# The query-key-value projection of each node tile done in slots inside the pooling stage of a two-layer graph network

## The reference

```python
h = jnp.maximum(_layernorm(x, axis=-1), 0.0)
x = x + _L0_gnn_ref(h, W1, w2, src, dst)     # pooling: a softmax per dst of tanh(h @ W1.T) @ w2 at src, weights for h[src]
h = jnp.maximum(_layernorm(x, axis=-1), 0.0)
x = x + _L1_gnn_ref(h, edge_index, edge_attr_16, ...)
# _L1: two TransformerConv layers (8 heads of 16, then 1 head of 128)
q, k, v = x @ Wq + bq, x @ Wk + bk, x @ Wv + bv
alpha = sum(q[dst] * (k[src] + e)) / sqrt(C)     # e = edge_attr @ We
out = segment_sum((v[src] + e) * softmax_per_dst(alpha)) + x @ Ws + bs
```

## Time and profile before

| what | us |
|---|---|
| median of 3 timed runs (10591.73 to 10635.79) | 10591.98 |
| span of the profiled execution | 7414.1 |
| time of the runs that lies outside such a span | 3177.9 |
| GpSimd busy in the span | 4576.5 |
| VectorE busy in the span | 4663.7 |
| TensorE busy in the span | 5718.3 |

### The profile page before, as it was taken

One profiled execution on the slowest core, in us unless ns is written; L12 is line 12 of the kernel. 1 busy time (PEld: TensorE's weight loads), 2 busy tenths in 40 slices (PEclk: granted clock), 3 DMA queues, 4 the chain that ended last, 5 costly groups with the idle time before them and its releaser, 6 DMA issues. The chain is left out here.

```text
span 7414.1 us, 172328 instructions
## 1 busy us (share of the span) xinstructions
PE 5718.3 (77%) x38285; PEld 4085.0 (55%) x38285; DVE 4663.7 (63%) x12926; ACT 3438.6 (46%) x8180; POOL 4576.5 (62%) x4707
## 2 busy tenths in 40 slices
PE   4555566666665688888888888856889999999998
PEld 3455555555542466666666666633555556666666
DVE  4444555555665788999999999933444555555542
ACT  3233333333443466666666666612444444444441
POOL 0777777777750477777666665502777777777630
PEclk7777878888986799999999999977999999999995
DMA  2334444444434666666655555534445555555532
GB/s 81 85 82 83 85 85 87 88 89 89 92 90 140 161 155 157 159 158 153 151 144 145 142 140 137 130 103 119 108 110 112 117 116 119 123 122 123 119 88 60
DMA packets 1267854, 861.45 MB, mean 116 GB/s; under 512 B 637234, under 2 KB 1158320, under 8 KB 1266840
## 3 DMA queue, kind: packets, MB, share of 16 engines
q1 hardware_dynamic: 1091672, 438.53, 25.3%
q0 software_dynamic: 175168, 411.90, 23.7%
HBM read 780.46 MB, written 69.42 MB: 115 GB/s over the span
## 5 line engine op out<-in xcount | busy, mean ns | idle before, releaser
L757 POOL DMA_INDIRECT ring_multi<-kv_rows,src_cols x1564 | 1609.3, 1029 | 1029.7 <-issue 440.4
L1155 POOL DMA_INDIRECT ring_single<-h_rows,src_cols x1564 | 1482.6, 948 | 857.2 <-issue 480.3
L1155 POOL DMA_INDIRECT ring_pool<-pool_rows,src_cols x1564 | 1482.0, 948 | 678.6 <-issue 451.5
L1258 PE MATMUL ps_s_pool<-ident,row_pool 128*128 128x128 f32 x1952 | 365.1, 319 | 718.0 <-ACT row_pool L1300 716.8
L1300 ACT ACTIVATE row_pool<-ring_pool 128x520 f32 x488 | 309.1, 633 | 1162.1 <-POOLq L1146 1162.1
L958 PE MATMUL ps_e_multi<-w_edge,attrT 64*128 64x512 f32 x976 | 544.5, 638 | 331.4 <-DVE kv L847 310.9
L1222 DVE CUSTOM_DVE_ANT_0 masked_pool<-mask_pool,ps_s_pool,start_pool 128x512 f32<-128x512 bf16 x488 | 364.8, 748 | 633.4 <-PE ps_s_pool L1258 552.3
L1271 PE MATMUL ps_p_pool<-row_pool,probT_pool 128*128 128x129 f32 x3904 | 667.1, 325 | 55.2 <-DVE probT_pool L1235 54.2
L847 DVE TENSOR_TENSOR kv<-ring_multi,ps_e_multi 128x1024 f32<-128x1024 f32 x488 | 596.1, 1222 | 161.6 <-issue 124.0
L1258 PEld LDWEIGHTS ps_s_pool<-ident,row_pool 128*128 128x128 f32 x1952 | 254.1, 160 | 801.5 <-issue 764.9
L1305 ACT ACTIVATE rowT<-ps_r 128x512 f32<-128x512 f32 x488 | 291.7, 598 | 816.4 <-PE ps_r L1265 816.4
(11 more groups left out here) (218 smaller groups left out, 12218.1 us busy)
## 6 DMA issues: line engine op xcount, KB each, us to landing
dst_pool<-in_dst_rows SPq DMA_DIRECT2D x488, 128.0 KB
dst_multi<-in_dst_rows SPq DMA_DIRECT2D x488, 128.0 KB
dst_single<-in_dst_rows SPq DMA_DIRECT2D x488, 128.0 KB
query_multi<-query_parts SPq DMA_DIRECT2D x488, 96.0 KB
cols<-query_cols SPq DMA_DIRECT2D x488, 64.0 KB
ring_pool<-pool_rows,src_cols POOLq DMA_INDIRECT x1564
ring_multi<-kv_rows,src_cols POOLq DMA_INDIRECT x1564
ring_single<-h_rows,src_cols POOLq DMA_INDIRECT x1564
```

What stands on the lines that cost most here:

```text
L757: pool.indirect_dma_start(out=ring[:, u, j, :], out_offset=None, in_=rows, in_offset=bass.IndirectOffsetOnAxis(ap=g.src_cols[:, c:c + 1], ...
L1155: pool.indirect_dma_start(out=ring[:, u, j, :], out_offset=None, in_=rows, in_offset=bass.IndirectOffsetOnAxis(ap=g.src_cols[:, c:c + 1], ...
L1258: i = T_.transpose(ps_s[p1][:, j * P:(j + 1) * P], row[:, u1, j, D + 1:D + 2].to_broadcast([P, P]), g.ident[:])
```

## The change

The projection no longer has a stage. `pool_stage` replaces `dense_stage("pool")`: the same items, with *slots* between them. A slot does one whole tile. There is a slot after every fourth item up to item 387 (97 slots), and one after every item from 390 to 487 (98 slots). Which tile a slot takes is worked out in `prepare`: the next one, if it is finished by then, else the last one again, or the unused 99th tile while none is finished; a slot does its full work in every case. The slot's work is spread over later steps: sums, statistics and `x` at two steps behind the slot's item, normalization at 5, turning at 7 and 9, product at 10, evacuation at 11, the query's parts at 11 and 14, the three stores at 23. The bias is added by a second product of 3 bfloat16 rows. The reciprocal root is an exponential of a logarithm. `skip` and `x1` are stored side by side, and the fold stage loads them with one DMA.

The diff, cut to its core (the removed `project_stage` stands above in full):

```diff
+SLOT_ITEMS = [*range(3, BLOCKS - 1, 4), *range(BLOCKS - 1, ITEMS)]
+TILE_SLOTS = len(SLOT_ITEMS)
+EARLY_SLOTS = len(range(3, BLOCKS - 1, 4))
+SLOT_XB = 4
+SLOT_OB = 16
@@ build
-        dense_stage(g, "pool", g.pool_rows, D + 2, 8)
-        project_stage(g)
+        slot_signals(g)
+        pool_stage(g)
@@ buffers
-    g.kv_rows = scratch("kv_rows", [NODES, 2 * D])
+    g.kv_rows = scratch("kv_rows", [SLOTS * P, 2 * D])
+    g.skip_x_rows = scratch("skip_x_rows", [SLOTS * P, 2 * D])
-    g.x1_rows = scratch("x1_rows", [NODES, D])
-    g.skip1_rows = scratch("skip1_rows", [NODES, D])
@@ prepare, vector: the tile of each slot
+            v.tensor_copy(tiles_done[0:1, 0:EARLY_SLOTS],
+                          item_t[0:1, 4:4 + 4 * EARLY_SLOTS].rearrange("a (s k) -> a s k", k=4)[:, :, 0])
+            v.tensor_copy(tiles_done[0:1, EARLY_SLOTS:TILE_SLOTS - 1], item_t[0:1, BLOCKS:ITEMS])
...
+            v.tensor_tensor_scan(turn[:], ones_slot[:], tiles_done[:], 0.0, ALU.add, ALU.min).then_inc(s_dve, 1)
...
+            v.tensor_copy(g.slot_tiles[:], turn[:]).then_inc(s_dve, 1)
@@ pool_stage: the items as in dense_stage, fully unrolled, with the parts below
+    LAST = ITEMS + 24
...
+        @block.sync
...
+                if has(n, ITEMS):
+                    E["mask"].wait(sp, n - U)
+                    sp.dma_start(dst[:, u], t["dst_rows"][ds(items.block(u), 1), :].to_broadcast([P, EDGES_B]))\
...
+                s = slot_at(n - 8)
+                if s is not None:
+                    tiles[s] = slot_tile(sp, s)
+                    F["x_sum"].wait(sp, s - SLOT_XB)
+                    sp.dma_start(xb[:, s % SLOT_XB], ...
+                s = slot_at(n - 23)
+                if s is not None:
+                    at = ds(tiles.pop(s), 1)
+                    rows_stored(sp, s - 1)
+                    F["x_sum"].wait(sp, s)
+                    F["kvs"].wait(sp, s)
+                    sp.dma_start(g.kv_rows..., out[:, s % SLOT_OB, D:3 * D]).then_inc(stored[s % 2], 16)
+                    sp.dma_start(g.skip_x_rows..., out[:, s % SLOT_OB, 3 * D:5 * D]).then_inc(stored[s % 2], 16)
+                    F["part2"].wait(sp, s)
+                    sp.dma_start(g.parts[D]..., parts[:, s % SLOT_OB]...).then_inc(stored[s % 2], 16)
...
+            def statistics(s):
...
+                tile = ds(slot_tile(dve, s), 1)
+                E["summed"].wait(dve, SLOT_ITEMS[s])
...
+                V.tensor_scalar(den[:, k], weight, 1e-30, None, ALU.max).then_inc(F["weight"].sem, 1)
+                F["weight"].wait(dve, s)
+                V.reciprocal(den[:, k], den[:, k]).then_inc(F["den"].sem, 1)
+                x_landed(dve, s)
+                rows_stored(dve, s - SLOT_OB)
+                F["den"].wait(dve, s)
+                V.scalar_tensor_tensor(out=x1, in0=sums, scalar=den[:, k], in1=x, op0=ALU.mult, op1=ALU.add)\
+                 .then_inc(F["x_sum"].sem, 1)
+                F["x_sum"].wait(dve, s)
+                V.bn_stats(stat[:, k], x1).then_inc(F["stats"].sem, 1)
+                F["stats"].wait(dve, s)
+                V.bn_aggr(agg[:, s % 8], stat[:, k]).then_inc(F["var"].sem, 1)
+
+            for n in range(LAST):
...
+                step(n, n % U)
+                s = slot_at(n - 2)
+                if s is not None:
+                    statistics(s)
+                s = slot_at(n - 5)
+                if s is not None:
+                    F["rstd"].wait(dve, s)
...
+                    V.tensor_scalar(normal[:, s % 2], out[:, s % SLOT_OB, 4 * D:5 * D], agg[:, s % 8, 0:1],
+                                    rstd[:, s % 4], ALU.subtract, ALU.mult).then_inc(F["normal"].sem, 1)
+                s = slot_at(n - 11)
...
+                    V.tensor_tensor(out=rest[:, s % 4], in0=out[:, s % SLOT_OB, 0:D], in1=parts[:, s % SLOT_OB, 0],
+                                    op=ALU.subtract).then_inc(F["rest"].sem, 1)
+                s = slot_at(n - 14)
...
+                    V.tensor_tensor(out=parts[:, s % SLOT_OB, 2], in0=rest[:, s % 4], in1=parts[:, s % SLOT_OB, 1],
+                                    op=ALU.subtract).then_inc(F["part2"].sem, 1)
@@ tensor, between the items' parts
+                s = slot_at(n - 7)
...
+                    T_.transpose(ps_h[:, 0:P], normal[:, s % 2], g.ident[:]).then_inc(F["turned"].sem, 1)
...
+                s = slot_at(n - 10)
...
+                    F["turned_sb"].wait(pe, s)
+                    F["kvs"].wait(pe, s - 1)
+                    T_.matmul(ps_z[:], hT[:, s % 4], w[:].rearrange("p a n -> p (a n)"), start=True, stop=False)
+                    T_.matmul(ps_z[:], ones3[:], bias_rows[:], start=False, stop=True).then_inc(F["product"].sem, 1)
@@ scalar, between the items' two exponentials and the copy of the gathered rows
+            act.preload_act_table_set("natural_log_exp_and_others")
...
+                s = slot_at(n - 9)
...
+                    S_.activation(hT[:, s % 4], ps_h[:, 0:P], ACT.Relu).then_inc(F["turned_sb"].sem, 1)
+                s = slot_at(n - 5)
...
+                    S_.activation(log[:, s % 4], agg[:, s % 8, 1:2], ACT.Ln, bias=g.ln_eps[:]).then_inc(F["log"].sem, 1)
+                    F["log"].wait(act, s)
...
+                    S_.activation(rstd[:, s % 4], log[:, s % 4], ACT.Exp, scale=-0.5).then_inc(F["rstd"].sem, 1)
+                s = slot_at(n - 11)
...
+                    F["product"].wait(act, s)
+                    rows_stored(act, s - SLOT_OB)
+                    S_.activation(out[:, s % SLOT_OB, 0:4 * D], ps_z[:], ACT.Copy).then_inc(F["kvs"].sem, 1)
+                    F["kvs"].wait(act, s)
+                    S_.activation(parts[:, s % SLOT_OB, 0], out[:, s % SLOT_OB, 0:D], ACT.Copy)\
+                     .then_inc(F["part0"].sem, 1)
+                s = slot_at(n - 14)
...
+                    S_.activation(parts[:, s % SLOT_OB, 1], rest[:, s % 4], ACT.Copy).then_inc(F["part1"].sem, 1)
@@ fold_stage, sync
-                    sp.dma_start(skip[:, u], rows_of(g.skip1_rows, n)).then_inc(loaded[u], 16)
-                    sp.dma_start(x1[:, u], rows_of(g.x1_rows, n)).then_inc(loaded[u], 16)
+                    sp.dma_start(skip_x[:, u], rows_of(g.skip_x_rows[0:NODES], n)).then_inc(loaded[u], 16)
```

More of the change, by code:

```diff
@@ L60 @@
 DEN_EPS = 1e-16
+SLOT_ITEMS = [*range(3, BLOCKS - 1, 4), *range(BLOCKS - 1, ITEMS)]
+TILE_SLOTS = len(SLOT_ITEMS)
+EARLY_SLOTS = len(range(3, BLOCKS - 1, 4))
+SLOT_OF = {item: s for s, item in enumerate(SLOT_ITEMS)}
+SLOT_XB = 4
+SLOT_OB = 16
+assert SLOT_ITEMS[EARLY_SLOTS:] == list(range(ITEMS - NODE_TILES, ITEMS))
 assert ITEMS % U == 0 and NODE_TILES % ROWS_B == 0 and BATCHES % 2 == 0
@@ L175, in buffers @@
     g.block_ends = sb(g, ctx, "block_ends", [1, 392], I32)
+    g.slot_tiles = sb(g, ctx, "slot_tiles", [1, TILE_SLOTS], I32)
     g.ident_b = sb(g, ctx, "ident_b", [P, P], BF16)
@@ L222, in prepare @@
         word = sb(g, ph, "word", [1, GROUPS])
+        tiles_done = sb(g, ph, "tiles_done", [1, TILE_SLOTS])
+        ones_slot = sb(g, ph, "ones_slot", [1, TILE_SLOTS])
+        turn = sb(g, ph, "turn", [1, TILE_SLOTS])
+        idle = sb(g, ph, "idle", [1, TILE_SLOTS])
         iota_ni = sb(g, ph, "iota_ni", [P, P], I32)
@@ L364, in _ @@
             v.tensor_scalar(g.fresh_tile[:], ps_b[:, 0:ITEMS], FAR, None, ALU.mult).then_inc(s_dve, 1)
+            v.tensor_copy(tiles_done[0:1, 0:EARLY_SLOTS],
+                          item_t[0:1, 4:4 + 4 * EARLY_SLOTS].rearrange("a (s k) -> a s k", k=4)[:, :, 0])
+            v.tensor_copy(tiles_done[0:1, EARLY_SLOTS:TILE_SLOTS - 1], item_t[0:1, BLOCKS:ITEMS])
+            v.memset(ones_slot[:], 1.0)
+            v.memset(tiles_done[0:1, TILE_SLOTS - 1:TILE_SLOTS], float(NODE_TILES)).then_inc(s_dve, 1)
+            dve.wait_ge(s_dve, done + 16)
+            v.tensor_tensor_scan(turn[:], ones_slot[:], tiles_done[:], 0.0, ALU.add, ALU.min).then_inc(s_dve, 1)
+            dve.wait_ge(s_dve, done + 17)
+            v.tensor_scalar(idle[:], turn[:], 0.0, float(NODE_TILES + 1), ALU.is_equal, ALU.mult).then_inc(s_dve, 1)
+            dve.wait_ge(s_dve, done + 18)
+            v.scalar_tensor_tensor(out=turn[:], in0=turn[:], scalar=-1.0, in1=idle[:], op0=ALU.add, op1=ALU.add)\
+             .then_inc(s_dve, 1)
+            dve.wait_ge(s_dve, done + 19)
+            v.tensor_copy(g.slot_tiles[:], turn[:]).then_inc(s_dve, 1)
         @block.tensor
@@ L442, in _ @@
                 D_["stats"].wait(sp, n - LOADS)
-                sp.dma_start(acc[:, n * ROWS_B:(n + 1) * ROWS_B, 0:D], rows_of(t["x"], n))\
+                sp.dma_start(acc[:, n * ROWS_B:(n + 1) * ROWS_B, 0:D], rows_of(t["x"][0:NODES], n))\
                   .then_inc(loaded[n % LOADS], 16)
@@ L1087, in dense_signals, with slot_signals @@
     g.flat = {k: Signal(sem(g, "flat_" + k)) for k in DENSE_SIGNALS}
+SLOT_SIGNALS = ("weight", "den", "x_sum", "stats", "var", "log", "rstd", "normal", "turned", "turned_sb", "product", "kvs", "part0",
+                "rest", "part1", "part2")
+def slot_signals(g):
```

(15 more changed lines are left out.)

404 lines of the change are left out of this document (245 added, 159 removed).

## The result

| | before | after |
|---|---|---|
| median of the timed runs, us | 10591.85 (4 runs) | 10905.15 (4 runs) |
| span of the profiled execution, us | 7414.1; in e1 10518.7 | 10887.8 |

The ratio is 1.031 (95% interval 1.026 to 1.036). The prediction was 10423.

The account below looks back on a forecast made before the run. The prediction took GpSimd's gathers to set the pooling stage's length, with VectorE narrowest in late items. Its terms, -297 + 78 + 49 + 8 - 10 + 3, summed to -169 us: 10423 us, range 10350 to 10560.

Parts of the forecast that it names:

- rival 5: Whole program: time outside the span grows with some 16,000 more instructions at 18 ns each, +290, 10713 us; chance 3%.
- (a): Removed projection stage: the time between its ends is saved, -297.1 us.
- (d): Drain after VectorE's last item in the pooling stage: 14 remaining stores at 3.5 us each, +49 us.
- (e): Tail of the last item and way from the last store's issue to the next stage's gather: +8 us.
- Rival 1: Late items and drain: the chain of stores becomes the bound, 6.2 us per item, +68, 10660 us; chance 9%.
- (b): Early 97 slots of the pooling stage: hidden under gathers of 4.95 us a block, 0 us.
- (c): Late 98 slots of the pooling stage: 4.3 us per item against 3.5 for the gathers, +78 us.
- Rival 2: Late items: the single product buffer couples TensorE and ScalarE, pushing the period to 5.0 us, 10492 us; chance 15%.
- (f): Fold stage: one DMA instead of two spares an issue in each of 14 batches, -10 us in all.
- (g): prepare: eight small VectorE operations are added, +3 us.
- (3): Late items: independent instructions overlap, so slots nearly fit with a period of 3.7 us, -236, 10356 us; chance 14%.
- (4): ScalarE in the slots: logarithm and exponential each load a table, 2.6 us a slot, +44, 10636 us; chance 2%.

Follow-up runs that it names:

- e1: The kernel before, profiled again with no edit: 10573.41 us, ratio 0.999, span 10518.7.
- e6: As e2, with TensorE's turn of a slot also one step later: 10500.89 us, ratio 0.993 against the kernel before.
- e7: The changed kernel with early slots that do full work but store nothing (first excepted), late slots doing all tiles: 10861.18 us, ratio 1.027.
- e3: The changed kernel without its early slots but one, the 98 late slots doing all tiles: 10801.16 us, ratio 1.020.
- e9: The kernel of e4 with the GpSimd pauses of e8 and 14 instead of 16 places for slot outputs: 9600.17 us, ratio 0.908.
- e10: The changed kernel as it is, with the GpSimd pauses of e8 in both stages: 10187.23 us, ratio 0.960.
- e8: The kernel before with five small waited-for GpSimd memsets ahead of each block of four gathers, pooling and one-head stages: 9939.75 us, ratio 0.940.
- e12: The kernel of e9 with one memset ahead of every gather instead of five ahead of every block: 9221.27 us, ratio 0.870.
- e2: The changed kernel with ScalarE's copy of the turned tile moved ahead of the step's exponentials: 10635.48 us, ratio 1.005 against the kernel before.
- e4: The changed kernel with late slots after every second item only, 49 instead of 98: 10409.53 us, ratio 0.983 against the kernel before.

## Why the prediction was wrong

**What bounds the kernel now.** "So the gathers set the length of the pooling stage" was read rightly from an execution that is not the one timed. The failure began in the sum: "The 3178 us between them have no row. I leave them unchanged." They lie in the stages that the change works in. The Trainium skill (Runtime: NRT & Kernel Launch, The ~15µs preamble/postamble breakdown) speaks of a gap of some 6 us between a profile's total and the measured time. The span here, from the first to the last instruction, is not that total, and it differs from the time of its execution by 2 us (10889.62 and 10887.8). A gap of 3178 should have been taken as a sign that the profile is of another regime, and not carried along as a constant. A rival for that was missing: rival 5 put those microseconds outside the span and let them grow with the program, and e1 has none there.

**(a), (d), (e).** Right: -231 for -240. From VectorE's last sum, as the prediction measured it, the hole goes from 296 to 42 us. After that sum 13 slots store, one every 2.8 us, below the 3.1 to 3.8 that I had. Rival 1, the chain of stores, is out: in e6 the same stores fit into a period of 6.0 us, and e7 without early stores is no shorter up to item 389.

**(b) Early slots.** Wrong: 0 forecast, 116 measured. The step's own words give the bound, "If that cover were gone it would cost at most 97 x 1.8 = 175", and the cover was gone: up to item 389 an item takes 6.0 us on average in e1, where it took 4.2 in the first trace. e3 and e7 show the price to be the engines' work, e9 and e10 show it to vanish once gathers pace the stage. By the Trainium skill (SBUF — State Buffer, Who interferes with whom), which the prediction weighed, VectorE's normalization could hold up GpSimd. The trace doesn't show it: 947 ns per gather with slots and 946 without, and 475.6 against 467.5 us of gaps without a known cause. What e8 and e12 show goes the other way: how GpSimd spaces its gathers decides whether TensorE's results come late. That section says of TensorE and ScalarE that they never wait on anyone, which is about ports; the late starts of e1 are on TensorE's results alone, and it doesn't cover them.

**(c) Late slots.** This is the step that failed, and the larger part: 98 x (4.3 - 3.5) = +78 against +492. I took the pitch as the busiest engine's own work plus hops, 4.3 us; it was 10.0. The other side of the term moved too: without slots a late item takes 5.0 us in e1, not the 3.5 of the earlier trace rows. VectorE's work was sized well (the slot and the item's mask, minimum, sum and copy are some 4.5 us of the 10.26). TensorE's was too small: 5.05 us for 3.8, read at a granted clock of 0.90 to 0.92 where the late items have 0.67, so that the slot's product takes 1.82 us on average and not 1.05. Neither comes near 10.0: the pitch was a ring over three engines in which that work is one part. Rival 2 was near: it named a single PSUM buffer between TensorE and ScalarE and ScalarE's order as the danger, with p = 5.0. It looked at the buffer of the product, and the one that bound was that of the turn. It added the work of TensorE and ScalarE and did not follow the ring on through VectorE. The Trainium skill (Perfetto Trace Analysis, Matmuls) advises that independent groups rotate through PSUM banks, so that the evacuation of one overlaps the next; e2 agrees so far as less coupling at this buffer took 280 us off. The pooling stage already holds eight PSUM buffers (two each for scores, turned weights and products, one each for turn and slot product), and a second one for the turn wasn't tried.

**(f), (g).** (f) is wrong in sign: +5 for -10. It took an issue off each batch and let the landing stay as it was; the one DMA of 896 KB lands a median of 5.7 us after its issue, where the second of two with 448 KB took 4.7. (g) is right: +3 for +3.

**Rivals 3 to 5.** That the late slots nearly fit (3) came out only in e9, with paced gathers and half of the slots. The whole trace after has five table loads, so none per slot (4). The page counts 8304 instructions more than before, not some 16,000, and they cost nothing outside the span (5).

## What to carry to other kernels

When a profile's span is not the time of the run, profile again before any term is worked out: which engine sets the length can differ between the two. When work goes into a software pipeline, write down for each wait which step of the other engine it waits for, and follow it round until it comes back: the pitch can't be shorter than the longest such ring divided by the steps that it spans, and moving one instruction in the program order can be worth more than the instruction. A single buffer that is handed over at every step is where to begin.

## What the runs showed of the hardware

- With back-to-back gathers by GpSimd (one per 1.25 us) TensorE's results were used late, 2.6 and 3.5 us in the rows of e1, and over 1 us in 293 of 1161 handovers of the pooling stage up to item 389. Handovers from VectorE or ScalarE were never over 0.15 us late there. Slowing the gathers to one per 1.55 us with an idle 128x256 memset ahead of each, in the pooling and the one-head stage, left none of the 293 and took 11% off the time (e4 10409.53, e12 9221.27; e12 has 14 places for slot outputs instead of 16). The mean of a gather did not change (946 to 955 ns). Why the results come late isn't shown: the records of semaphore changes are incomplete in these traces. The eight-head stage, which gathers too, was not given pauses.
- One profiled execution of the kernel before had none of this: a span of 7414.1 with gathers as long, and one late start in the pooling stage. None of the timed runs, 10520 to 10640 us, was like it, and what set it apart stays open.
- One load of 896 KB landed 5.7 us after its issue, the second of two loads of 448 KB 4.7 us (medians of 14 in after and before): joining them made the stage 5 us longer.
